# All 21 weight pieces loaded and split in the front stage, none left for batch 0

## The reference

```
xn = layernorm(x)
attention: q = xn @ w_q.T (16 heads of 32), k, v = xn @ w_kv.T (one head, shared),
           rotary positions, causal softmax, out @ w_proj.T + b_proj
ffn:       shared = relu(xn @ up.T)**2 @ down.T           (512 -> 1024 -> 512)
           routed = fc2(sum over the 8 chosen of 32 experts of cw * w2(relu(w1(fc1(xn)))**2))
out = x + attention + shared + routed
```

## Time and profile before

| | us |
|---|---|
| median of 3 runs | 1720.31 (1719.22 to 1723.76) |
| profiled execution | 1720.09 |
| its span | 1718.3 |
| TensorE busy | 1616.7 (94%) |
| VectorE busy | 1184.0 (69%) |
| ScalarE busy | 1092.5 (64%) |
| GpSimd busy | 825.9 (48%) |

### The profile page before, as it was taken

The page is one execution under the profiler, slowest core; times in us unless marked ns, Lnnn a source line. Parts: engine busy times, 40 slices in busy tenths (PEclk is TensorE's granted clock), DMA queues, the critical chain, the costliest instruction groups (busy, mean ns, idle before and its releaser), DMA issues.

```text
span 1718.3 us, 40612 instructions
## 1 busy us (share of the span) xinstructions
PE 1616.7 (94%) x10811; PEld 1383.5 (81%) x10811; DVE 1184.0 (69%) x3611; ACT 1092.5 (64%) x2852; POOL 825.9 (48%) x673
## 2 busy tenths in 40 slices
PE   5787889999999999999999999899999999999999
PEld 4776667777787787787778777799999999999987
DVE  6779777867777778678687777355555555555567
ACT  3368765757757756667577567366666666666642
POOL 0213023435524534345244253377777877778760
PEclk9899899999999999999999999999999999999999
DMA  7954614434434444344343345499999999998794
GB/s 276 394 168 143 106 52 139 138 109 140 133 102 151 141 120 139 109 152 139 97 152 121 123 133 153 113 184 191 187 194 181 191 189 200 197 174 160 137 267 177
DMA packets 193090, 273.71 MB, mean 159 GB/s; under 512 B 37400, under 2 KB 133791, under 8 KB 190820
## 3 DMA queue, kind: packets, MB, share of 16 engines
q0 software_dynamic: 60352, 92.59, 25.1%
q1 hardware_dynamic: 77572, 113.01, 23.1%
q10 hardware_dynamic: 54944, 65.52, 12.8%
HBM read 121.83 MB, written 129.67 MB: 146 GB/s over the span
## 4 chain that ended last, share of the span: by engine, by line
PE 68%; DVE 16%; issue 7%; ACT 4%; DMA 4%; DVEq 1%; SPq 0%; ACTq 0%; POOL 0%; POOLq 0%
PE e_psH L1729 14%; PE e_psY L1740 14%; DVE m_sc L1108 5%; PE m_psO L1358 4%; PE e_psX L1714 4%; PE m_psU L64 3%; PE m_psT L1336 3%; PE m_psS L1311 3%; PE m_psU L66 3%; PE m_psU L65 3%; PE m_psY L64 3%; PE m_psY L65 3%; PE m_psY L66 3%; DVE m_sc L1120 2%; ACT m_sc L942 2%
## 5 line engine op out<-in xcount | busy, mean ns | idle before, releaser
L1694 POOL DMA_INDIRECT sums<-e_y,e_where x287 | 445.9, 1554 | 156.0 <-issue 91.5
L864 POOL DMA_INDIRECT slot_rows<-m_row,slots x256 | 267.0, 1043 | 461.5 <-ACT m_sc L942 428.9
L942 ACT ACTIVATE m_sc<-m_sc,m_low 128x512 f32<-128x512 f32 (+3 forms) x512 | 283.5, 556 | 126.4 <-DVE m_low L1108 124.7
L1729 PE MATMUL e_psH<-e_xt,e_w_of 128*128 128x128 f32 x2296 | 305.0, 276 | 3.3 <-ACT e_xt L1589 3.3
L1740 PE MATMUL e_psY<-e_w,e_ht 128*128 x1148 | 295.8, 380 | 1.3 <-ACT e_ht L1600 1.2
L1108 DVE CUSTOM_DVE_ANT_0 m_sc<-m_psS,cst 128x512 f32<-128x512 f32 (+3 forms) x512 | 229.8, 485 | 91.9 <-PE m_psS L1311 89.9
L1729 PEld LDWEIGHTS e_psH<-e_xt,e_w_of 128*128 128x128 f32 x2296 | 280.3, 192 | 3.7 <-ACT e_xt L1589 3.5
L1595 ACT ACTIVATE e_w_of<-e_w 128x512 f32 x287 | 180.9, 630 | 119.4 <-issue 115.5
L1740 PEld LDWEIGHTS e_psY<-e_w,e_ht 128*128 128x128 f32 x1148 | 196.4, 191 | 17.0 <-issue 2.1
L1311 PE MATMUL m_psS<-m_ks,m_qs 96*128 96x256 f32 (+2 forms) x512 | 158.6, 369 | 42.4 <-DVE m_low L1108 35.1
L1650 DVE TENSOR_SCALAR e_where<-e_row,e_shifts 128x1 uint32<-128x1 uint32 x287 | 61.4, 214 | 196.8 <-DMA sums<-e_y,e_where 178.4
(11 more groups left out here) (235 smaller groups left out, 3245.4 us busy)
## 6 DMA issues: line engine op xcount, KB each, us to landing
e_row<-slot_rows ACTq DMA_DIRECT2D x287, 144.5 KB, 3.4
m_qs<-m_qhi SPq DMA_DIRECT2D x256, 64.0 KB, 2.0
e_w<-in_w SPq DMA_DIRECT2D x256, 64.0 KB
f_xt<-in_x SPq DMA_DIRECT2D x8, 1024.0 KB, 11.5
m_qs<-m_qlo SPq DMA_DIRECT2D x128, 64.0 KB, 2.0
m_res<-in_x SPq DMA_DIRECT2D x8, 1024.0 KB, 6.4
sums<-empty POOLq DMA_DIRECT2D x32, 256.0 KB
partial<-m_res ACTq DMA_DIRECT2D x16, 512.0 KB
```

Of the source, the lines that this page charges most:

```text
L864: pool.indirect_dma_start(out=xs, out_offset=bass.IndirectOffsetOnAxis(ap=slots_sb[:, g, k:k + 1], axis=0), in_=row[g % 2][:, :], in_offse ...
L942: nc.scalar.activation(cols, cols, ACT.Exp, bias=low[:, h % 2, i:i + 1], scale=-1.0, accum_out=total[:, h % 2, i:i + 1]).then_inc(exp_done, 1)
L1694: pool.indirect_dma_start(out=both_sums, out_offset=bass.IndirectOffsetOnAxis(ap=where[u % NY][:, 0:1], axis=0), in_=y[u % NY][:, :], in_o ...
L1729: mm = pe.matmul(psH[u % 2][:, k * P:(k + 1) * P], w1_of[u % 2][:, c * INTER + k * P:c * INTER + (k + 1) * P], xt[u % 2][:, c * P:(c + 1) ...
```

## The change

Only the table changes. With it 21 pieces instead of 12 are issued in the front's steps: 1, 3, 4, 4, 5 and 4 for the groups 2 to 7, where it was 0, 2, 3, 3, 4 and 0. SyncE has none left to load after the front, and ScalarE's loop over pieces in batch 0 is empty, since PIECES_OF[-1][1] is 21. The order of the pieces stays.

```diff
-PIECES_A_GROUP = (0, 0, 0, 2, 3, 3, 4, 0)
+PIECES_A_GROUP = (0, 0, 1, 3, 4, 4, 5, 4)
 PIECES_A_SLOT = 2
 PIECES_OF = [(sum(PIECES_A_GROUP[:n]), sum(PIECES_A_GROUP[:n + 1])) for n in range(B)]
 UNDER_WAY = 5
```

## The result

The changed kernel took 1732.99 us (median of 4 runs, 1730.54 to 1735.24), the kernel before 1719.76 us on the same chip (1719.16 to 1723.76). The ratio is 1.0067, with a 95% interval of 1.0053 to 1.0081. The change makes the kernel slower by 0.67%. The forecast was 1724.3 us with a range of 1718.5 to 1728.5: the sign was right, the size was not. The profiled execution took 1735.24 us (span 1733.4), 15.1 us more than the one of before.

The account below looks back on a forecast made before the run. The front was taken as bound by what is queued ahead of each x load, batch 0 by VectorE and ScalarE, then TensorE. Front +3.3 and batch 0 +0.7 made +4.0 us: 1724.3 us, range 1718.5 to 1728.5.

Parts of the forecast that it names:

- The front, loads: Front: five more pieces ahead of the last x load on full DMA queues delay it by 3.3 us.
- D: Rival, front loads: queues have more room, three pieces are absorbed, 3.3 becomes 1.3, 1722.3 us; chance 0.10.
- The front, splitting: Front: ScalarE's copies and GpSimd's subtractions there cost nothing on the path, up to 1 us at the upper end.
- rival C: Front: subtractions meet the normalisations of groups 5 and 7 too, 3.9 us a meeting on VectorE, 1728.2 us; chance 0.10.
- Batch 0, what arrives: Batch 0's start: the earlier clearing makes ScalarE's last latents store land in 10.1 us; ScalarE starts 5.9 us later.
- 1.3 us to start and signal: Last latents store beside the clearing: the start and signal part of its about 10.1 us landing.
- Rival B: Last latents store: the clearing is drained first, ScalarE delayed 10.8 us, 1729.1 us; chance 0.11.
- A: Rival, last latents store: not held up by the clearing, all 4.0 us gained, 1719.6 us; chance 0.17.
- Batch 0, what goes: Batch 0: copies leaving ScalarE and subtractions no longer stretching VectorE gain 4.0 us, taken alone.
- The stacked queries' moves: Batch 0: small moves land in 3.0 us instead of 2.0 beside the clearing, behind the same wait: nothing.

Follow-up runs that it names:

- kernel 4: Changed kernel with the clearing after the latents' stores and GpSimd's subtractions held until after the normalisation: 1720.63 us, ratio 0.9993 to the kernel before.
- kernel 7: Kernel before with only SyncE's loads by the new table, and GpSimd's subtractions held until after the normalisation: 1722.60 us, ratio 1.0016.
- kernel 6: Kernel before with only SyncE's loads by the new table, copies, subtractions and clearing by the old one: 1729.08 us, ratio 1.0038.
- kernel 1: Changed kernel, but GpSimd waits for the latents' stores to land before it clears slot_rows' tail: 1724.82 us, ratio 1.0020 to the kernel before.
- kernel 3: Changed kernel with the clearing cut into eight parts, each issued after the one before has landed: 1722.34 us, ratio 1.0018 to the kernel before.
- kernel 2: Kernel before with only the clearing moved into the front, after GpSimd's 12th piece: 1732.77 us, ratio 1.0065.
- kernel 8: Kernel before with the table (0, 0, 0, 2, 3, 3, 4, 4), four pieces behind the last x load: 1729.93 us, ratio 1.0050.
- kernel 5: Kernel before with only GpSimd's subtractions held until after the normalisation: 1721.59 us, ratio 1.0006.
- kernel 11: Kernel 4 with the table (0, 0, 1, 3, 3, 3, 5, 6), two pieces fewer ahead of the last x: 1723.42 us, ratio 1.0018 to the kernel before.

## Why the prediction was wrong, step by step

Four terms were mis-sized: the meetings in the front, put at nothing on the path (3.0 us on the chain), TensorE's clock, left out (1.8 us), the start of the last store of latents beside the clearing, put at 1.3 us with the signal (about 5 us to its first packets), and, through the first two, the front as a whole (9.5 us instead of 3.3).

**The front, loads: right where the subtractions are held.** Forecast +3.3 us, statistics at 86.6 us. Measured 86.57 in kernel 4 and 86.35 in kernel 7, where the subtractions are held, and 86.01 in kernel 6, where they aren't. In the changed kernel they begin at 87.94 us, outside my 85.7 to 87.5. Kernels 1 and 3 have the same front as the changed kernel to the last instruction, and there they begin at 89.29 and 86.49 us. Single executions of one front thus lie 2.8 us apart, and whether meetings also make the last x late isn't shown. Bytes ahead of the last load of x over the rate of the full queues gave the right size; so did the count of SyncE's issues (3.6 us), and no run tells the two apart. D, with 1.3 us, is out.

**The front, splitting: failed.** I gave it nothing on the path and up to 1 us. I had looked up each meeting in a group where VectorE waits for x afterwards, and found it hidden there: in the changed kernel VectorE still waits 1.46 us for x after the 4.89 us at 80.17. I didn't put the same question to the last group, behind which no load of x follows. Its normalisation is on the chain, and it takes 4.89 us instead of 1.91. With the 4.7 us of x that is 7.7, and the last store of latents was issued 9.5 us late, not 3.3. The four copies behind it, 2.2 us longer, are not on the chain, which goes from the normalisation to TensorE. I did have rival C, but let it need meetings in groups 5 and 7; the one in group 7 is enough. And I said that in the profile they just miss each other: kernel 6 shows that 3 us of delay of x make them meet, with no subtraction moved by its table. My own first term triggered the second.
The page "SBUF — State Buffer" of the Trainium skill (section "SBUF: two separate sides") says that the side which starts first keeps the shared ports for the whole instruction and the other blocks. The trace agrees in this: 1.9 us became 3.92 or 4.89, in steps of about 1 us per subtraction. Its condition for VectorE, two SBUF inputs or a fast mode, is one on which these rows say nothing further.

**TensorE's clock: left out.** The missing 1.8 us are TensorE's. Before, it came to the last group's turning (L257) without a pause and worked on at a granted clock of 1.00 (2.4 GHz). In the changed kernel it waits for one tile after the other, and by 98 us it works at 0.50 (1.2 GHz). First before, then changed:

```profile
91.25 1.94 PE L257 MATMUL f_pt<-cst,f_xn 128*128 128x128 f32 x16
```

```profile
93.00:99.60 6.60, 6.59 (x50) 6.35 (x48) 3.26 (x7) 4.31 (x10) 4.92 (x4) 1.00 0.98 301
```

```profile
95.93 0.63 PE L257 MATMUL f_pt<-cst,f_xn 128*128 128x128 f32 x4 [2.77 <-DVE f_xn L307]
...
100.18 1.11 PE L257 MATMUL f_pt<-cst,f_xn 128*128 128x128 f32 x4 [0.29 <-DVE f_xn L307]
```

```profile
101.00:104.00 3.00, 3.00 (x15) 3.00 (x14) 3.00 (x7) 2.07 (x4) 1.51 (x2) 0.50 0.29 113
```

The matmuls of the front (f_pf) follow each other every 0.24 us until 104.2 us and every 0.13 us after it; from the end of the turning to the copy before the first of the two stores it is 7.9 us instead of 6.4. Kernel 7, where no normalisation is stretched, shows the same by itself: x is 3.1 us late, the last store 4.7, and the clock is 0.50 from 96 to 98 us. In kernel 4 TensorE waited once, 2.0 us, kept 1.00, and the front is 3.3 us longer, x and nothing else. So the 4.6 us between kernels 1 and 4 hold some 2 us of clock (kernel 1: x 6.0 us late and 3.0 us of normalisation, but a first exponential 11.0 us late). These are single traces; how often an execution loses this clock isn't known.

**Batch 0, what arrives: the mechanism half right, the size not.** The clearing followed the last subtraction by 2.2 us as forecast (2.1), at 116.67 instead of 110.8 us, because the front was longer. The store then landed in 15.5 us, not 10.1. The term that failed is "1.3 us to start and signal". The DMA view of the changed kernel by stretches (123 to 127, 128 to 129, 131 to 135 us; queue, packets, MB, share; q0 is GpSimd's, q10 ScalarE's, q1 SyncE's):

```profile
q0 software_dynamic: 236, 1.09, 87.4%
q1 hardware_dynamic: 105, 0.15, 13.6%
...
q10 hardware_dynamic: 30, 0.03, 9.5%
...
q0 software_dynamic: 242, 1.05, 74.7%
q10 hardware_dynamic: 240, 0.25, 19.6%
```

From 131 to 135 us it is packet by packet, as I had it. But from 123 to 127 us the store, already issued, gets not one packet; 4 come from 127 to 128 and 30 in the next microsecond. It gets going about 5 us after its issue. In the kernel before, its queue had moved this many in the stretch from 114 to 115 us, within 1.7 us of the issue:

```profile
q10 hardware_dynamic: 234, 0.24, 68.7%
```

5 us of start in place of about 0.8 (its first packets before) makes 10.1 into 14.3, near the 15.5. In kernel 2 it repeats: none of q10 from 113 to 117 us, then 25 packets in 2 us, and in step from then on. The page "DMA: Bandwidth & Descriptors" of the Trainium skill (section "Queues, rings and completion order") has each DMA engine take turns between the queue rows, a packet at a time. The trace agrees from 129 us on and does not before it. That what is already queued of the clearing must go first would explain it, and the 18 packets beside 142 in kernel 3 fit; neither this nor where such packets stand is shown. SyncE's q1 does get packets in those 4 us, so it is not all that stands still.
Rival B, with its threshold at a start of 129 us, thus came to pass in time (138.41 us) but only half in its mechanism: the clearing went first for some 4 us, and then the two took turns. A is out.

**Batch 0, what goes: right, a little small.** Forecast 4.0 us alone, 5.3 on ScalarE's road behind the late store. From the first exponential to slot 4 the changed kernel gains 5.5 us; kernels 1, 3 and 4, where no store is late, gain 5.1, 5.0 and 5.1 instead of 4.0. The instruction that took 1.37 us in the earlier trace rows takes 0.43 in VectorE's timeline of the changed kernel. The further 1.5 us between slots 4 and 9 is no part of it: kernel 2, with all nine pieces still in batch 0, has 0.7 of it, and kernel 1, with none, has nothing. Steps of 1 to 2 us up and down between later slots are in most of the kernels; I haven't traced them.

```profile
155.40 0.43 DVE L492 TENSOR_TENSOR ot<-ot 128x256 f32<-128x256 f32 x1
```

**The stacked queries' moves: hidden, as said, in the changed kernel only.** Each of the two in the row below took SyncE 1.8 us to issue, where SyncE needed 1.25 us for two at 108.01 us before, and VectorE's first scores waited 7.15 us behind such moves, beside ScalarE's wait for the store. I gave nothing, and that held here. In kernel 8, where no store hides them, they cost 9.2 us.

```profile
127.30 3.54 SPq L787 DMA_DIRECT2D m_qs<-m_qhi  x2
```

**The sum by ratios.** Collision +8.1 us (after against kernel 1), meetings +4.6 (kernel 1 against 4), the loads less batch 0's gain -1.2 (kernel 4 against before, an interval that holds zero): 11.5 us. I had 5.9, then 0, then 3.3 less 5.3: 3.9, and 4.0 with the rounding. The second term holds TensorE's clock as well. The chance of 0.31 for slower was too small: B, C and the forecast were weighed as if only one could happen, but they add up, and a late x brings C about.

## What to carry over

A piece of work that follows the moved one in an engine's program order moves with it: look up where the large transfer behind it will now be issued, and which short transfer someone waits for will be standing behind it. Issue such a filler in parts, each after the last has landed, or behind the short one. A meeting of two engines that is hidden in every group but the last is not hidden; and when the bounding load is late, work that just missed each other no longer does. Look also at what the late work does to TensorE: here it came back from its waits at half the granted clock, and 1.8 us went there.

## What the runs showed of the hardware

- A store issued on ScalarE's queue 6 us after a single 4.48 MB clearing had none of its packets moved for about 4 us and landed after 15.5 us (17.6 in kernel 2); with the same clearing in parts of 578 KB, each issued after the last had landed, it landed in 4.9 us, nearly all of it between two parts.
- Issuing a 64 KB move took SyncE 0.6 us before and up to 1.9 us while the clearing was moving, and in kernel 8 the move took up to 9 us.
- Four copies of 128x32 on VectorE took 2.59 us beside GpSimd's subtractions, 0.43 us without: the meeting costs by the instruction, not by its size.
- TensorE's granted clock was 0.50 after waits of 2.77, 0.80 and 0.45 us for the tiles of one normalisation (changed kernel), and after single waits of 4.55 us (kernel 5) and 7.23 us (kernel 11); after one of 2.60 us it was 1.00 first and 0.50 from 96 us (kernel 7); after one of 2.03 us it stayed at 1.00 (kernel 4). At 0.50 the matmuls of 128x288 followed each other every 0.24 us, at 1.00 every 0.13.
- Single executions of kernels 6 and 11 lay up to 12 and 7 us apart (1721.03 to 1733.18, 1719.37 to 1726.5), those of the kernel with the hold alone 3.3.
